# Recurrent sandwich kernel: the first x tile is normalized ahead of the bias and of the second tile

## The reference

```
u  = ln(x) @ W_in.T + b_in                       # 512 -> 1024
s_t = tanh(u_t + s_(t-1) * gamma + beta)         # 1024 steps over the sequence
x1 = x + ln(s @ W_out.T + b_out)                 # 1024 -> 512
f  = silu(ln(x1) @ q(gate_w) * gate_scale) * (ln(x1) @ q(up_w) * up_scale)   # 512 -> 1536
out = x1 + ln(f @ q(down_w) * down_scale)        # 1536 -> 512
```

## Time and profile before

| | us |
|---|---|
| three executions | 568.47, 562.3, 567.22 |
| their median | 567.22 |
| the profiled execution | 563.53 |
| its span, first to last instruction | 561.7 |
| PE busy | 541.0 (96%) |
| DVE busy | 446.2 (79%) |
| ACT busy | 375.3 (67%) |
| POOL busy | 248.3 (44%) |

### The profile page before, as it was taken

How to read it: one execution, slowest core, us unless ns; L and a number is a source line. 1 busy time by engine, 2 the same in 40 slices (tenths; PEclk the granted TensorE clock), 3 DMA queues, 4 the chain that set the end, 5 groups by cost and what they waited for, 6 DMA issues and landing times.

```text
span 561.7 us, 11945 instructions
## 1 busy us (share of the span) xinstructions
PE 541.0 (96%) x2960; PEld 457.7 (81%) x2960; DVE 446.2 (79%) x2606; ACT 375.3 (67%) x2315; POOL 248.3 (44%) x372
## 2 busy tenths in 40 slices
PE   6998989899999999999999999999999999999994
PEld 4946768789789888898888888988888797899993
DVE  3588999998797899877997898878987998875314
ACT  2587586865678776876677767876687677752322
POOL 1022365573846633761438234553343243535531
PEclk9999989999999999999999999999999999999998
DMA  8589499981024100120003000300002000200011
GB/s 274 201 256 237 133 201 190 255 136 57 13 47 151 58 2 2 56 78 2 1 2 112 21 1 2 102 13 2 2 1 76 1 2 1 76 3 1 1 39 37
DMA packets 25301, 39.92 MB, mean 71 GB/s; under 512 B 3728, under 2 KB 8464, under 8 KB 25232
## 3 DMA queue, kind: packets, MB, share of 16 engines
q1 hardware_dynamic: 19888, 30.24, 16.3%
q0 software_dynamic: 4608, 8.39, 9.1%
q10 hardware_dynamic: 736, 0.54, 0.3%
HBM read 26.57 MB, written 4.20 MB: 55 GB/s over the span
## 4 chain that ended last, share of the span: by engine, by line
PE 74%; DVE 16%; ACT 4%; DMA 2%; issue 2%; POOL 1%; ACTq 0%; POOLq 0%; DVEq 0%
PE gate_up L1108 27%; PE wide L1064 17%; PE wide L1134 13%; PE wide L1033 13%; DVE recur L1213 5%; DVE peaks L1410 3%; DVE powers L1393 2%; ACT pairs L1531 2%; DVE rounders L1400 1%; PE wide L1084 1%; DMA raw_own<-rounders 1%; PE wide L995 1%; DMA cols<-gamma 1%; DVE fused L1335 1%; DVE stats_x L1218 1%
## 5 line engine op out<-in xcount | busy, mean ns | idle before, releaser
L1524 ACT ACTIVATE pairs<-recur 128x8 f32<-128x8 f32 x768 | 137.1, 178 | 91.2 <-DVE recur L1204 90.7
L1204 DVE TENSOR_TENSOR_SCAN recur<-recur,pairs 128x16 f32<-128x16 f32 x768 | 150.8, 196 | 50.4 <-ACT pairs L1524 47.8
L1524 ACT ACTIVATE pairs<-recur_second 128x8 f32<-128x8 f32 x768 | 136.8, 178 | 0.0
L1204 DVE TENSOR_TENSOR_SCAN recur_second<-recur_second,pairs 128x16 f32<-128x16 f32 x768 | 132.9, 173 | 0.0
L1713 POOL TENSOR_TENSOR fused_lo<-fused,fused_hi 128x256 fp32r<-128x256 f32 x95 | 70.0, 738 | 132.3 <-ACT fused_hi L1575 132.2
L1064 PE MATMUL wide<-w_out_sb,pairs 128*128 128x512 f32 (+1 forms) x272 | 112.9, 562 | 0.1
L1033 PE MATMUL wide<-x_norm_t,w_in_sb 128*128 128x256 f32 x448 | 102.0, 383 | 2.0 <-ACT x_norm_t L1475 1.5
L1033 PEld LDWEIGHTS wide<-x_norm_t,w_in_sb 128*128 128x128 f32 x448 | 85.2, 192 | 15.1 <-ACT x_norm_t L1475 2.1
L1064 PEld LDWEIGHTS wide<-w_out_sb,pairs 128*128 128x128 f32 x272 | 75.2, 298 | 24.2 <-issue 0.2
L1559 ACT ACTIVATE gated<-gate_up,gate_scale_cols 128x128 f32<-128x128 f32 (+1 forms) x168 | 63.4, 379 | 29.2 <-PE gate_up L1108 28.7
L1134 PE MATMUL wide<-down_q,fused_hi 128*128 128x512 f32 x192 | 81.4, 424 | 0.4 <-POOL fused_lo L1713 0.2
(11 more groups left out here) (134 smaller groups left out, 798.5 us busy)
## 6 DMA issues: line engine op xcount, KB each, us to landing
x_res<-x SPq DMA_DIRECT2D x16, 256.0 KB, 3.3
x_in<-x SPq DMA_DIRECT2D x15, 256.0 KB, 4.7
out<-z SPq DMA_DIRECT2D x14, 256.0 KB, 2.5
x_norm_t<-x_t SPq DMA_DIRECT2D x5, 512.0 KB, 3.3
raw_own<-rounders POOLq DMA_DIRECT2D x9, 256.0 KB, 4.9
w_in_sb<-w_in_t SPq DMA_DIRECT2D x4, 512.0 KB, 7.3
w_out_sb<-w_out_t SPq DMA_DIRECT2D x8, 256.0 KB, 5.4
raw_own<-down_w SPq DMA_DIRECT2D x8, 256.0 KB, 4.0
```

Source lines behind the costliest of these rows:

```text
L1204: eng.tensor_tensor_scan(preact_of[b].rearrange("p c k -> p (c k)"), factors_of[b].rearrange("p c k -> p (c k)"), pairs[:, t % RING, colum ...
L1524: ins = eng.activation(pairs[:, t % RING + 1, columns, 0], preact_of[b][:, :, 1], ACT.Tanh)
```

## The change

The load of x for block 0 is cut by tiles: SP and ACT each issue two DMAs (tile 0, then tile 1) of half the size instead of one, and each tile has a semaphore of its own. On DVE tile 0 is now normalized directly behind its statistics, then tile 1 is measured, then comes the bias, then tile 1 is normalized. On PE the transposes of tile 1 go from ahead of the first products to between the column groups m = 1 and m = 2 of tile 0's products; on ACT the copies of tile 1 go among the copies of u, and the wait for the bias goes to just ahead of the first of these. The waits for `s_x_in` of later blocks count one block less.

```diff
@@ -497,8 +497,8 @@
 HEAD = -60.0
-FIRST = {"x_half": ((0, 1), (4, 5)), "x_whole": (2, 6), "x_norm": (7, 9), "t1": (20, 21), "t1_copy": (22, 23),
-         "first_u": (26, 28, 30, 32), "first_u_copy": (29, 31, 33, 35)}
+FIRST = {"x_half": ((0, 1), (7, 8)), "x_whole": (2, 9), "x_norm": (5, 12), "bias": 11, "t1": (20, 29), "t1_copy": (22, 32),
+         "first_u": (26, 28, 30, 32), "first_u_copy": (31, 33, 35, 37)}
@@ -659,6 +659,7 @@
+        s_first_x_in = [sem(f"s_first_x_in{g}") for g in range(batch)]
@@ -866,7 +867,8 @@
                 yield HEAD
-                eng.dma_start(x_in[0:P:batch, :, :], x_blocks[0][0]).then_inc(s_x_in, 16)
+                for g in range(batch):
+                    eng.dma_start(x_in[0:P:batch, g, :], x_blocks[0][0][:, g, :]).then_inc(s_first_x_in[g], 16)
                 eng.dma_start(ident[:, :], identity).then_inc(s_ident_in, 16)
@@ -1171,7 +1173,7 @@
             def prepare_bias():
-                yield HEAD + 3
+                yield HEAD + FIRST["bias"]
@@ -1226,8 +1228,10 @@
-                        if h == 0:
-                            eng.wait_ge(s_x_in, 16 * batch * (n + 1))
+                        if h == 0 and n == 0:
+                            eng.wait_ge(s_first_x_in[b], 16 * batch)
+                        elif h == 0:
+                            eng.wait_ge(s_x_in, 16 * batch * n)
@@ -1442,7 +1446,8 @@
                 yield HEAD - 1
-                eng.dma_start(x_in[1:P:batch, :, :], x_blocks[0][1]).then_inc(s_x_in, 16)
+                for g in range(batch):
+                    eng.dma_start(x_in[1:P:batch, g, :], x_blocks[0][1][:, g, :]).then_inc(s_first_x_in[g], 16)
@@ -1452,7 +1457,7 @@
                 eng.activation(warm[:, 0:1], warm[:, 1:2], ACT.Silu)
-                yield HEAD + 1
+                yield HEAD + FIRST["first_u_copy"][0] - 0.5
                 eng.wait_ge(s_bias, 1)
```

## The result

| | before | after |
|---|---|---|
| executions | 7, 562.3 to 568.47 | 7, 560.5 to 561.96 |
| median us | 566.27 | 561.38 |
| profiled execution us | 563.53 | 561.96 |
| its span us | 561.7 | 560.2 |

The ratio is 0.9927, with a 95% interval of 0.9899 to 0.9954: 4.1 us less (2.6 to 5.7), within the 1% that was called no change. But the two profiles differ by 1.6 us only, the medians by 4.9, and the changed kernel's executions lie within 1.5 us where those of before were spread over 6.2. (Three slow executions of this study are left out throughout: one of each kernel at over 2500 us, and one of the kernel before at 573.32 us with a mean granted clock of 0.94.)

A forecast was written before the change was run, and what follows sets the result against it. PE is 96% busy, so only its idle time, mostly the head behind gamma's load, can shrink. First scan 8.8 + 7.86 + 0.46 = 17.1 against 19.23, 2.1 us earlier: 567.2 - 2.1 = 565.1, range 560.0 to 568.5.

The forecast's parts named there:

- the gap between profile and median: Whole kernel: the median stands 3.7 us above the profiled execution, so 561.4 profiled becomes 565.1.
- What bounds the head: Head: the chain of waits begins with gamma's load, landing at 8.02; tile 0 waits 2.4 us for nothing of its own.
- Tile 0's path: Head: x lands at 4.4, normalization starts at 6.4, and x alone allows a first product at about 8.2.
- other rule, on disjoint partition halves: Load of x: two transfers to disjoint partition halves serialize over the same engines, so one transfer is better.
- The warm-up as a bound: PE's head: warm-up products last until 7.11 and hold tile 0's transposes by at most 0.2 us.
- w_in_sb at 8.75: First products on PE: the first weight group lands at 8.75 and sets the first product at 8.8 (8.5 to 9.0).
- a sign of being wrong: Tile 0's products: the prediction is wrong if a column group of w_in_sb stops PE for more than some tenths.
- Transposes in the stream 0.46: PE, among tile 0's products: tile 1's four transposes add 0.46 us before the first scan, upper bound 0.76.
- The parts at nothing: Late bias, tile 1's copies on ACT, DVE's weight step and SP's later release cost nothing; covers 1.5 to 2.8 us.
- The end follows the start: After the head: no event after 20 us is tied to a fixed time, so 2.1 us arrive in full.
- rival (d): Recurrence: SP's late release makes DVE wait for block 1's x; landing at 26 gives 568.7; chance 0.03.
- rival (c): PE's clock falls at another place after idle time: 563.8 without this fall, 566.4 with a second; chance 0.10.

The follow-up runs named there:

- filled kernel: Kernel before with 6 warm-up products instead of 4 and filler products of zeros in PE's idle time in the head: 565.05 us, ratio 0.9968.

## Why the prediction was right or wrong

The range and the sign held: 561.38 lies in 560.0 to 568.5, and the change is within 1%. The size was wrong: 2.1 us forecast, 4.1 measured by the ratio (2.6 to 5.7 by its interval, 4.9 by the medians). Two steps failed: the gap between profile and median, carried over as a constant, and the warm-up's end, taken as fixed. The second was made up for by luck.

- **What bounds the head: right.** Gamma at the front of the chain, with tile 0 ready behind it; the experiment with only the bias moved (and ACT's wait for it) brings the whole gain.
- **Tile 0's path: mis-sized, then covered.** Landing 3.36 instead of 4.4; the half loads took about 2.6 us, less than either bound (3.3 and 4.0). Cutting the load brought tile 0 1.4 earlier, more than my rows allowed (0.7). The fit of the Trainium skill, DMA: Bandwidth & Descriptors, section on the anatomy of one DMA, would have it 0.3 earlier; the trace differs, and the measurement decides. That section gives the fit for DMAs that GpSimd issues, and these come from SP and ACT. The prediction's other rule, on disjoint partition halves, doesn't bear on the cut either, which is by tiles: both kernels load the two batch rows into separate partitions. But nothing came of it: the warm-up stood in front.
- **The warm-up as a bound: the term that failed in the head.** I took its end, 7.11, from one profile as fixed and let it hold the transposes by 0.2. It held them by 2.2. The warm-up's halves start 0.85 apart until the clock rises and 0.43 apart then, and it rose at another moment: the trace's first record of the clock begins at 5.41 before and at 7.70 after. With eight halves the warm-up ended at 6.7 to 8.3 in the profiles.
- **w_in_sb at 8.75: wrong as the cause, near in time.** It landed at 7.6 in the changed kernel's first profile and wasn't waited for; in the second the first product did wait for it, until 8.61. That idle time of 1.4 us is more than the some tenths which the prediction had named as a sign of being wrong. The first product at 9.15 and 8.61 frames the forecast 8.8, which is luck: in the first profile the warm-up held it about as long as the weights had been thought to.
- **Transposes in the stream 0.46: right,** 0.44. First scan 17.1: measured 17.55 and 16.97.
- **The parts at nothing: right.** Nothing on the chain waited for the late bias (DVE stood 2.0 us until gamma was there at 9.07, but PE took tile 1 at 12.82 without a wait), DVE did not wait for the x of block 1, SP was released at 13.46 (forecast 13.1).
- **The end follows the start: right,** by the line above. (In rival (d), x landing at 26 gives 568.8, not 568.7; nothing rests on it.) A second fall of the clock (104 to 112 us, granted 0.79 in the changed kernel, 1.00 before) cost nothing that can be seen at the end; before, PE had waited 0.84 us for DVE in this stretch.
- **Where the missing 2 us were: rival (c), at a place I had excluded.** I noted that the profiled execution stood 3.7 us below the median, and carried this as a constant onto the changed kernel. It was no constant: 2.7 us before with all executions (566.27 against 563.53), and -0.6 after. PE's idle time of 2.5 us in the head of before lets the clock fall in some executions (by the times and mean clocks, in most), which costs tile 0's transposes and products 0.8 to 2.8 us in the four profiles with 2.5 to 3.6 us of idle that show it; the change leaves no idle time over 1.4 us in the head, and neither of its two profiles has a fall there. I had written that this idle time "had no such fall behind it", from the one execution that I could see. The idle time was in my own rows, and so was the price of a fall, 1.3 us for 16 products.

How the 4 us divide is known roughly. Order: gamma off the chain moves the first scan from 19.2 (19.5 with gamma at its usual 8.3) to 17.0 to 17.6, about 2.2 us. Clock: filling the idle time without touching the order gave 1.8 us by its ratio (1.0 to 2.7), if anything too little, because the fillers delayed the first product by 0.2 us. Together 4.0, beside the 4.1 measured; the first is read from single profiles, so the agreement is no proof. That the fall comes from the idle time, and not from what else the orders change, rests on the filled kernel and on the profiles with 2.5, 2.7, 2.8 and 3.6 us of idle. Of the five profiles with an idle time of 2.48 us and more at one place in the head, four show a fall and one, the first of before, doesn't; of the nine with less, only that with two warm-up products does. How much idle time it takes stays open: with 1.0 us in the profile (six warm-up products) some executions were still high, and those have no profile of their own, while the partly filled kernel had 1.4 us and no high execution.

## What to carry to other kernels

A small load that gates a vector engine can stand at the front of everything: put what it feeds behind all work that doesn't need it. An idle time of the matmul engine costs twice where the products behind it are on the chain, once as waiting and once, in some executions, as a lower clock; a kernel whose executions scatter and whose profile is below its median asks for a second profile before its waits are priced. The mean granted clock of each execution, held against its time, hints at this without one, but it doesn't say where the clock was low: the changed kernel had 0.991 in its profile at 561.96 us, with its falls at 79 and 107 us, where none cost anything that can be seen.

## What was not expected of the hardware

- The same head of the same kernel ran its first products at both levels of the clock in two profiles, with 2.56 and 2.48 us of idle ahead: 56 products in 6.42 and in 6.92 us, and the transposes of tile 0 and 1 in 1.43 and 2.21 us of PE time.
- The warm-up of eight halves, always begun at 1.48, ended at 6.70 to 8.25: its own length depends on when the clock rises (first record at 4.58 to 7.70 us), by 1.5 us.
- Four loads of 128 KB instead of two of 256 KB brought the first tile at 3.4 to 3.5 instead of 4.7 to 5.1, and gamma, issued one DMA later, at 8.5 to 9.7 instead of 7.1 to 8.9 (without the kernel that loads tile 1 later still).
